# Second Mamba: the product of u and B one state ahead of the scan on VectorE

## The reference

```
deltaA = jnp.exp(delta[..., None] * A)
dBu = delta[..., None] * Bm[:, :, None, :] * x_c[..., None]
def step(h, t):
    dA_t, dBu_t, C_t = t
    h = dA_t * h + dBu_t
    y = jnp.einsum('bdn,bn->bd', h, C_t)
    return (h, y)
y = (y + x_c * Dp) * jax.nn.silu(z)
return y @ out_proj_w.T
```

## Time and profile before

| | us |
|---|---|
| median of 3 runs | 3366.28 |
| lowest and highest run | 3365.24, 3376.97 |
| the profiled execution | 3369.36 |
| its span in the trace | 3367.6 |
| TensorE busy | 2981.9 (89%) |
| VectorE busy | 2391.1 (71%) |
| ScalarE busy | 2001.3 (59%) |
| GpSimd busy | 881.5 (26%) |

### The profile page before, as it was taken

How to read it: one execution, slowest core, us unless ns; L and a number is a source line. 1 busy time by engine, 2 the same in 40 slices (tenths; PEclk the granted TensorE clock), 3 DMA queues, 4 the chain that set the end, 5 groups by cost and what they waited for, 6 DMA issues and landing times. The chain is left out here.

```text
span 3367.6 us, 43971 instructions
## 1 busy us (share of the span) xinstructions
PE 2981.9 (89%) x14254; PEld 1851.8 (55%) x14254; DVE 2391.1 (71%) x5307; ACT 2001.3 (59%) x3426; POOL 881.5 (26%) x971
## 2 busy tenths in 40 slices
PE   7998889898999997789887777788999998799998
PEld 5766233233777663256553333354677766677776
DVE  5665777785555776678766888867777777577776
ACT  4442667676444446645446667634577876377786
POOL 1020433422000001210003776720133332033332
PEclk9999999999999998899998889999999999799999
DMA  2000111220100330023333222224311010001111
GB/s 88 1 18 23 63 60 62 75 63 31 34 1 0 118 99 10 0 71 99 101 116 104 90 85 79 91 72 129 99 51 45 32 48 7 19 29 51 43 34 54
DMA packets 117868, 193.37 MB, mean 57 GB/s; under 512 B 18396, under 2 KB 31132, under 8 KB 117512
## 3 DMA queue, kind: packets, MB, share of 16 engines
q1 hardware_dynamic: 116056, 187.68, 17.7%
q10 hardware_dynamic: 1584, 2.88, 0.2%
HBM read 172.23 MB, written 18.25 MB: 57 GB/s over the span
## 5 line engine op out<-in xcount | busy, mean ns | idle before, releaser
L420 POOL TENSOR_TENSOR norm_rstd<-norm_rstd,minus_half 128x4 f32<-128x4 f32 (+1 forms) x136 | 176.6, 1298 | 1192.1 <-DVE norm_rstd L407 1181.7
L2532 ACT ACTIVATE main_tiles_r<-banks,feature_cols 128x512 fp32r<-128x512 f32 x512 | 352.6, 689 | 187.9 <-PE banks L262 166.3
L2540 DVE TENSOR_TENSOR main_tiles_r<-main_tiles,main_tiles_r 128x512 fp32r<-128x512 f32 x512 | 383.5, 764 | 67.9 <-ACT main_tiles L2533 66.1
L986 DVE TENSOR_REDUCE gate_scratch<-banks 128x2 f32<-128x1024 f32 (+2 forms) x320 | 344.9, 1114 | 96.1 <-PE banks L251 66.0
L1146 ACT ACTIVATE main_tiles<-banks 128x512 f32<-128x512 f32 (+1 forms) x608 | 315.3, 582 | 133.7 <-PE banks L1127 91.6
L260 PE MATMUL banks<-normed_pairs,moe_weights 128*128 128x512 f32 x740 | 368.5, 498 | 13.3 <-ACT main_tiles L2533 6.5
L2577 POOL TENSOR_TENSOR normed<-normed,main_tiles 128x512 f32<-128x512 f32 x128 | 217.7, 1701 | 532.7 <-DVE main_tiles L2566 532.7
L2533 ACT ACTIVATE main_tiles<-banks,feature_cols 128x512 f32<-128x512 f32 x512 | 349.7, 683 | 0.0
L260 PE MATMUL banks<-main_tiles_r,moe_weights 128*128 128x512 f32 x700 | 308.1, 440 | 32.3 <-DVE main_tiles_r L2540 26.7
L262 PE MATMUL banks<-normed_pairs,moe_weights 128*128 128x512 f32 x740 | 292.4, 395 | 0.0
L261 PE MATMUL banks<-normed_pairs,moe_weights 128*128 128x512 f32 x740 | 292.1, 395 | 0.0
(11 more groups left out here) (374 smaller groups left out, 6682.9 us busy)
## 6 DMA issues: line engine op xcount, KB each, us to landing
main_tiles<-gates_d SPq DMA_DIRECT2D x400, 256.0 KB, 3.3
mamba_tiles<-c_rows_d SPq DMA_DIRECT2D x92, 256.0 KB, 3.4
spare_nat<-c_rows_d SPq DMA_DIRECT2D x36, 256.0 KB, 3.3
found_d<-main_tiles SPq DMA_DIRECT2D x32, 256.0 KB, 2.0
parts_d<-bf_parts SPq DMA_DIRECT2D x48, 128.0 KB, 1.8
q_stacks<-parts_d SPq DMA_DIRECT2D x192, 32.0 KB
k_stacks<-parts_d SPq DMA_DIRECT2D x192, 32.0 KB
weight_staging<-in_w SPq DMA_DIRECT2D x22, 256.0 KB, 3.8
```

What stands on the lines that cost most here:

```text
L420: eng.tensor_tensor(rstd[:, k, 1, 0:w], rstd[:, k, 0, 0:w], minus_half[:, 0:w], ALU.pow).then_inc(s.norm_pow)
L986: eng.tensor_reduce(o.rearrange("p (n s) -> p s n", s=2)[:, :, j0:j0 + per], psum[:, b0:b0 + 2, 0:per * (k1 - k0)].rearrange("p s (n c) -> ...
L2532: eng.activation(pair_3(j)[0], psum[:, 2 + j % 2, :], ACT.Relu, bias=bias)
L2540: eng.tensor_tensor(lo, h3_of(j), hi.bitcast(F32), ALU.subtract).then_inc(s.m3_lo)
```

## The change

Three due times change. The product comes due 1.9 us earlier, at -1.6, and so stands ahead of the preceding state's scan, which is due at 1.4 - 2.75 = -1.35. The spread comes due half a microsecond earlier. The whole second Mamba, with all that is tied to it, is placed 2 us later against the last chunk of the expert stage before it, which keeps the first product at 22.4 after that chunk's begin (22.3 before). No instruction, wait, tile or bank is added or removed.

```diff
-    T_MB = m2_at[-1] - 24.0
+    T_MB = m2_at[-1] - 22.0
...
     def pe_state_zb(eng):
-        for q, i, n, when in state_items(-3.2):
+        for q, i, n, when in state_items(-3.7):
...
     def dve_state_db(eng):
-        for q, i, n, when in state_items(0.3):
+
+        for q, i, n, when in state_items(-1.6):
             yield when
             if n == 0:
                 eng.wait_ge(*mb_dve(i, "u"))
             eng.wait_ge(s.st_zb, q + 1)
             eng.tensor_tensor(zb_of(q), zb_of(q), u_of(i), ALU.mult).then_inc(s.st_db)
```

## The result

| | before | after |
|---|---|---|
| median of 15 runs, us | 3369.56 | 3381.04 |
| lowest and highest run | 3363.28, 3376.97 | 3372.68, 3387.35 |
| the profiled execution | 3369.36 | 3375.2 |
| its span | 3367.6 | 3373.5 |

The changed kernel is slower: ratio 1.0042, with 95% interval 1.0034 to 1.005. By the ratio that is 14 us; the medians lie 11.5 us apart. The forecast was 3363 with a range to 3379; the median lies above the range.

What follows compares the result with a forecast made beforehand. VectorE was taken to bound chunks 0, 1 and 7, a chain through other engines chunks 2 to 6. Savings 0.7 + 1.5 + 1.3 = 3.5 us gave 3365.9, or 3363 on the median's scale; forecast 3357 to 3369, full range 3350 to 3379.

Steps and rivals of the forecast that it cites:

- The saved gap of 0.17 us: On VectorE, scans no longer directly follow their own product; 83 gaps of 0.17 us, 14.1 us at most.
- Rival D: VectorE's reordering saves no gap, by the Trainium skill's rule; +5.8 us, 3372; chance 0.15.
- Late spreads at the sixth, eighth and ninth state: Products there wait for TensorE's spread: waits rise from 14.6 to some 30 us, scans' waits fall from 17.0.
- Nothing pays for that: Chunk 5, sixth state: the fifth scan, pushed from 2063.44 to 2066.86, costs nothing; the sixth scan waits for its exponential.
- The walk: Step-by-step forecast of chunk 5's new order; -0.14 us, applied to chunks 2 to 6 for 0.7 us.
- The convolution waits for ScalarE as before: Chunk 5, behind the sixth state: the convolution's wait for ScalarE is unchanged; no cost given.
- From there to the end of the chunk two gaps net are saved: Chunk 5, from behind the statistics to the chunk's end: 0.34 us saved.
- The three full chunks: Chunks 0, 1 and 7: 1.9 us saved, 1.2 lost at the ninth scan; net 0.5 or more each, 1.5 together.
- The spread half a microsecond sooner: TensorE's spread crosses three neighbours per chunk; costs nothing while a wait for GpSimd stands, else 0.6 us per chunk.
- T_MB, -1.3 us: Seam with the last expert chunk: L2061 passes the first scan, third spread waits under 2 us; between -2.5 and +2.
- Rival C: Slower: three scans per chunk pushed behind late spreads delay GpSimd and TensorE's sums; 15 us, 3381; chance 0.2.
- The stretch behind the last scan: Sign: the prediction is wrong if the part after the last scan changes by itself.

Runs made afterwards that it cites:

- e12: Changed kernel with the products of n = 6 to 10 and 12 back in their old place; 3370.2 against 3368.23 us, ratio 1.0009.
- e9: Changed kernel with the products of n = 6 and n = 12 back in their old place; 3369.51 against 3368.23 us, ratio 1.0009.
- e6: Changed kernel with the product of n = 12 (thirteenth state) alone back in its old place; 3372.86 us, ratio 1.0014.
- e7: Kernel before with the product of n = 12 (thirteenth state) alone moved ahead; 3367.21 us, ratio 0.9999.
- e10: Kernel before with the product of n = 6 (seventh state) alone moved ahead; 3366.03 us, ratio 0.9998.
- e4: Changed kernel with the products of the sixth, eighth and ninth state back in their old place; 3377.75 against 3365.76 us, ratio 1.0034.
- e13: Kernel before with all products of chunks 0 and 1 moved ahead; 3371.54 against 3369.23 us, ratio 1.0011.
- e14: Kernel before with only the last chunk's products moved ahead; 3372.39 us, ratio 1.0012.
- e1: Kernel before with only the product 1.9 us earlier, spread and T_MB as before; 3377.05 against 3365.76 us, ratio 1.0038.
- e3: Kernel before with only the spread half a microsecond earlier; 3365.41 against 3365.76 us, ratio 1.0004.
- e2: Kernel before with only T_MB 2 us later; 3366.86 against 3365.76 us, ratio 1.0.
- e5: Changed kernel with the products of n = 0, 2, 7, 12 and 15 back in their old place; 3373.24 against 3366.22 us, ratio 1.0024.
- e8: Changed kernel with the products of n = 0, 2, 5, 7, 8, 12 and 15 back in their old place; 3379.57 us, ratio 1.0038.

## Why the prediction was wrong, step by step

**The cost, from nested runs.** Five kernels of the table stand in a row in which each differs from the next by one set of products (e12 from before also by the two shifts), so their cycles can be subtracted: e12 less before -0.10; with the eighth to eleventh moved as well (e9 less e12) +0.36; with the seventh (e6 less e9) +0.43; with the thirteenth (after less e6) +0.44. Sum +1.13 us per middle chunk. The first of these is the saved gaps. It comes near to the -0.14 forecast, but by another sum: the forecast was 0.34 saved less 0.2 lost with all sixteen products moved, and here ten are. The other three are what the prediction had at nothing. Their sizes depend on the order in which the sets are added: alone in the kernel before, the thirteenth cost 0.29 (e7) and the seventh 0.40 (e10).

- **The saved gap of 0.17 us: right.** In after 106 scans start before the product in front of them has ended, by 0.08 to 0.10 us in the rows above; in before none does. Rival D is out. The Trainium skill's sentence ("VectorE: DVE Perf Modes", section "The DRAIN you can't avoid") that the semaphore costs nothing extra is about a row of copies; for a pair that depends on each other the rows here show a cost.
- **Late spreads at the sixth, eighth and ninth state: right in place,** and with the seventh behind them (waits of 2.15, 1.28, 1.44 and 2.09 us in chunk 5). The size was not: products wait 54.5 us, not some 30. The fall of the scans' waits was right (17.0 to 1.7).
- **"Nothing pays for that": the step that failed.** I followed the pushed fifth scan to the sixth on VectorE, where a wait of 2.62 us took it up, and stopped there. The walk itself has the sixth scan 0.41 us later (2070.0 instead of 2069.59), since the seventh product passes it, and puts that at nothing. Measured, it starts 0.44 us later behind its exponential. The scan's other user is GpSimd, and behind GpSimd's addition hangs L2287 and then z: 0.43 us per chunk (e6 less e9). "The convolution waits for ScalarE as before" is true of L2283 (1.11 us in after) and wrong of L2287 behind it, which ends only with GpSimd's addition. Its row in before had 0.57 us on one column, and its end within 0.02 us of GpSimd's; I had not asked why it was that long.
- **"From there to the end of the chunk two gaps net are saved": failed.** The walk looked at scans and statistics and overlooked L2294, which a product passes. That product (0.59 us in e7) lengthens the chain through ScalarE; part comes back later in the cycle (0.31 in e7).
- **The eighth to eleventh: the third term, 0.36 us.** It falls between z and L2294. By the rows of after GpSimd comes later there and TensorE's sums wait for it; that this is the path is argued, and only the size is shown. The set holds the products of the eighth and ninth state, two of the three that e4 kept in place without a gain, so how it divides is open.
- **The walk used chunk 5, which is slipped.** Its measured change, -0.17, agrees with the -0.14 of the walk, and means nothing. A chunk was chosen without asking whether its neighbour with the same list differed, and at what clock.
- **The three full chunks, -0.5 us each: wrong in two.** Chunk 0 gave -0.48, chunk 1 +1.12 (e13), chunk 7 +1.29 (e14). In chunk 7 VectorE is the fullest engine, and a product that waits for its spread (e14's rows) now keeps a ready scan from running; little idle time follows that could absorb it. One such loss of 1.2 us, at the ninth state, was in the sum; e14 shows three waits of about its size, and VectorE's idle time in the chunk rose from 1.6 to 3.7 us. In after itself chunks 0, 1 and 7 changed by -0.38, -0.10 and +3.67 us. Why chunk 1 lost nothing there is open: in e1, with all products moved too, it is 44.47 us, 1.42 longer than in before.
- **The spread half a microsecond sooner, nothing: right** (e3, 1.0004).
- **T_MB, -1.3 us: right in size.** The stretch from the first L2016 to the first scan lost 1.3 us, 0.6 of it within the expert chunks ahead of the last one (144.15 to 143.52 us), of which the prediction had no word. With T_MB alone (e2) it lost 2.0. L2061 stands ahead of the first scan, and the third spread waits 2.06 us for it, a little over the 2 named. VectorE and TensorE in after, beside the earlier trace rows:

```profile
1809.95 0.68 DVE L2061 TENSOR_TENSOR x_res<-banks,x_res 128x512 f32<-128x512 f32 x1
1811.14 1.21 DVE L2385 TENSOR_TENSOR_SCAN mamba_tiles<-mamba_tiles,banks 128x512 f32<-128x512 f32 x1
```

```profile
1810.69 0.39 PE L2364 MATMUL banks<-mamba_tiles,pick_bf 96*128 96x512 bf16 x1 [2.06 <-DVE x_res L2061]
```

- **Rival C** had the sign and, by accident, the number (3381). Its link, a scan that releases GpSimd too late, is one of those found; its place, the three pushed scans, is not (e4), and it had no word on L2294.

**What it sums to.** Middle chunks 5 x 1.13 = 5.7, ends -0.5 + 1.1 + 1.3 = 1.9, the stretch in front -1.3: 6.3 us (5.1 if chunk 1 counts as in after). The medians differ by 11.5 us, and no run accounts for the rest. What the record says of it has to do with the clock:

- The stretch behind the last scan, which the prediction named as a sign of being wrong if it changed, is 2.2 us longer in after (209.5 to 211.7) and 1.9 in e14 (211.4), against 208.6 to 208.9 in e2, e3, e7 and e13. By and large it goes with the time at 1.2 GHz within it: 20.5 us in before, 23.9 in after, 23.0 in e14, 17.1 in e2, e3 and e13.
- Each run lists its mean granted clock. It is 0.957 on average in the 15 runs of after and 0.959 to 0.960 in the runs of before that list one; on one and the same chip it is 0.9586 in e1 and 0.9600 in before. Within a kernel, an execution is longer by about 0.26 us for each us more at the low clock (a fit over all runs that list it). From these numbers my estimate is 3 to 5 us of the 11.5, the stretch behind the last scan partly included.
- In the profile of after, slips cost by estimate 2.1, 1.6 and 2.4 us in chunks 3, 6 and 7 (against 51.50 us in chunk 4, 50.01 in e1 and 36.71 in e14), in before 1.3 in each of two.

Whether the new order itself brings more time at the low clock stays open. So does e12: shorter cycle, no shorter time. Also open is why keeping more products in place made e5 and e8 worse between L2265 and z (26.3 us, against 26.05 in e6).

## What to carry to other kernels

An order on one engine is read by what each instruction releases on the others: for every step that a moved instruction passes, list its users, and carry on until the chain closes on itself, since a wait nearby that absorbs the delay for one user does nothing for the next. Idle time of an engine (8 us per chunk here) is no room for an extra instruction ahead of the few steps that lie on the closing chain. When stages repeat, compare those at equal clock on their chain, and divide the cycle into links by marks that both kernels have: links told here within 0.05 us what totals couldn't tell within 3.

## What the runs showed of the hardware

- **A step on one column was held by GpSimd.** L2287, 128 x 1 with two inputs in SBUF, took 0.57 or 1.00 us, according to when GpSimd's addition ran, and ended 0.01 to 0.02 us after it in all eight places of before and after; done on ScalarE it took 0.39 us and the cycle lost 0.49. L2283 ahead of it, with one of its two inputs in PSUM, took 0.75 us in both kernels. The Trainium skill names a second SBUF read interface that an operation with two SBUF inputs shares with GpSimd ("VectorE: DVE Perf Modes", section "Two Vector instructions with no wait between them"); the rows agree with such sharing, but that section gives it no cost, and no run here tells this cause from another.
- **The same hold lies on L2300,** the addition that makes delta, 128 x 512 with both inputs in SBUF. It takes 0.68 us in chunk 0, where nothing of GpSimd runs beside it, and 0.95 to 1.74 us in chunks 1 to 7 of before and after, each time ending 0.55 us after GpSimd's addition. L2294, with one input in PSUM, keeps its 0.67 to 0.69 us beside the same kind of GpSimd instruction. Chunk 5 of before, then of after; whether the 0.19 us more are on the chain, no run tells:

```profile
2099.42 1.26 POOL L2418 TENSOR_TENSOR mamba_tiles<-mamba_tiles 128x512 f32<-128x512 f32 x1
...
2099.81 1.43 DVE L2300 TENSOR_TENSOR mamba_tiles<-mamba_tiles 128x512 f32<-128x512 f32 x1
```

```profile
2096.67 1.26 POOL L2419 TENSOR_TENSOR mamba_tiles<-mamba_tiles 128x512 f32<-128x512 f32 x1
...
2096.87 1.62 DVE L2300 TENSOR_TENSOR mamba_tiles<-mamba_tiles 128x512 f32<-128x512 f32 x1
```

- **A dependent pair on VectorE** costs 0.17 us more than an independent one, with 83 such pairs in the stage.
- **The low clock** took 85.3 us of the stage in before and 92.2 us in after. Chunks 4 and 5 of after, at 0.91 and 0.93 of full clock, have equal links, and chunks that differ in where it fell differ by 1.3 us and more. TensorE's busy time in after by stretch, chunks 4 and 5:

```profile
1998.00:2048.00 50.00, 39.23 (x123) 17.93 (x123) 41.10 (x78) 33.31 (x61) 32.91 (x28) 0.91 0.27 85
2048.00:2100.00 52.00, 40.78 (x126) 18.13 (x124) 43.11 (x80) 35.31 (x67) 34.38 (x28) 0.93 0.25 82
```
